# Storing both gates of a token behind its normalised row and fetching them with the gathered row

## The reference

```
x = x + xattn(layernorm(x), ctx, ctx)     # 16 heads of 16, causal without the diagonal
x = x + ffn(layernorm(x))

# ffn: 8 experts, top 2 per token, 512 places per expert
scores = softmax(xt @ wg);  topv, topi = top_k(scores, 2)
topv = topv / sum(topv)                    # the two gates of a token
pos = place of (choice, token) in its expert's queue; valid = pos < 512
disp[topi, pos] += xt * valid
y = relu(disp @ w1 + b1) @ w2 + b2         # per expert, 256 -> 1024 -> 256
out = sum over the two choices of gate * y[topi, pos]
```

## Time and profile before

| | |
|---|---|
| median of three runs | 444.01 us (443.96 to 444.91) |
| profiled execution | 440.71 us |
| its span, first to last instruction | 438.6 us |
| mean granted clock of PE | 0.944 |
| PE busy | 372.2 us (85%), 3042 instructions |
| DVE busy | 292.2 us (67%), 616 instructions |
| ACT busy | 188.9 us (43%), 257 instructions |
| POOL busy | 221.8 us (51%), 306 instructions |
| DMA | 36199 packets, 49.10 MB |

### The profile page before, as it was taken

How to read it: one execution, slowest core, us unless ns; L and a number is a source line. 1 busy time by engine, 2 the same in 40 slices (tenths; PEclk the granted TensorE clock), 3 DMA queues, 4 the chain that set the end, 5 groups by cost and what they waited for, 6 DMA issues and landing times. The chain is left out here.

```text
span 438.6 us, 8178 instructions
## 1 busy us (share of the span) xinstructions
PE 372.2 (85%) x3042; PEld 317.5 (72%) x3062; DVE 292.2 (67%) x616; ACT 188.9 (43%) x257; POOL 221.8 (51%) x306
## 2 busy tenths in 40 slices
PE   3769898989999998876325899999999999999991
PEld 3647586868676766655213799999999998989891
DVE  6676776767676766526564857786776768677840
ACT  4424555555555553552240625344352626262310
POOL 7669766666657563351528703627180817250532
PEclk9988999999999999998655999999999999999997
DMA  8882725151606092214105403728090918230223
GB/s 222 235 235 73 202 61 159 51 169 41 177 8 189 3 240 64 74 73 157 48 1 174 162 2 107 194 63 239 13 272 16 269 31 244 58 46 12 30 31 35
DMA packets 36199, 49.10 MB, mean 112 GB/s; under 512 B 5022, under 2 KB 32064, under 8 KB 35136
## 3 DMA queue, kind: packets, MB, share of 16 engines
q1 hardware_dynamic: 27520, 34.91, 26.7%
q0 software_dynamic: 6144, 8.30, 10.0%
q10 hardware_dynamic: 2496, 5.38, 3.9%
HBM read 27.57 MB, written 8.39 MB: 82 GB/s over the span
## 5 line engine op out<-in xcount | busy, mean ns | idle before, releaser
L1391 POOL DMA_INDIRECT out_dram<-Y,scatter_idx x32 | 51.4, 1605 | 104.0 <-DVE Y L1541 88.3
L1434 ACT ACTIVATE hr<-ps,b_sb 128x512 f32<-128x512 f32 x64 | 43.4, 687 | 101.6 <-PE ps L1601 66.9
L682 DVE TENSOR_REDUCE nm<-ps 128x2 f32<-128x512 f32 (+1 forms) x96 | 61.5, 682 | 16.0 <-remote 10.5
L1611 PE MATMUL ps<-w_hi,h_hi 128*128 128x256 f32 x224 | 63.9, 285 | 1.2 <-DVE h_lo L1509 1.2
L1611 PE MATMUL ps<-w_lo,h_hi 128*128 128x256 f32 x224 | 63.4, 283 | 0.0
L1611 PE MATMUL ps<-w_hi,h_lo 128*128 128x256 f32 x224 | 63.4, 283 | 0.0
L489 ACT ACTIVATE PT<-ps 128x1536 f32<-128x1536 f32 x32 | 46.5, 1452 | 23.5 <-PE ps L936 22.6
L1507 DVE CAST h_hi<-hr 128x512 fp32r<-128x512 f32 x60 | 29.9, 499 | 38.8 <-ACT hr L1434 38.5
L1601 PE MATMUL ps<-XT_hi,w_hi 128*128 128x512 f32 x128 | 51.4, 402 | 1.5 <-DVE XT_lo L1500 1.5
L1601 PE MATMUL ps<-XT_hi,w_lo 128*128 128x512 f32 x128 | 51.2, 400 | 0.0
L1601 PE MATMUL ps<-XT_lo,w_hi 128*128 128x512 f32 x128 | 50.6, 395 | 0.0
(11 more groups left out here) (206 smaller groups left out, 880.6 us busy)
## 6 DMA issues: line engine op xcount, KB each, us to landing
raw<-in_L_ffn_w_dram SPq DMA_DIRECT2D x12, 1024.0 KB, 8.1
raw<-in_L_ffn_w_dram ACTq DMA_DIRECT2D x4, 1024.0 KB, 5.6
Ks<-k_h SPq DMA_DIRECT2D x24, 128.0 KB, 3.0
Qs<-q_h SPq DMA_DIRECT2D x24, 128.0 KB, 2.7
c_sb<-in_ctx_dram SPq DMA_DIRECT2D x8, 256.0 KB, 3.9
Ks<-k_m SPq DMA_DIRECT2D x16, 128.0 KB, 2.8
Qs<-q_m SPq DMA_DIRECT2D x16, 128.0 KB, 2.5
xn_rows<-x2n SPq DMA_DIRECT2D x8, 256.0 KB, 2.5
```

Source lines behind the costliest of these rows:

```text
L682: dve.tensor_reduce(nm[:, tile, h:h + count], max_bank[u % 2].rearrange("p (h j) -> p h j", h=count), AX_X, ALU.max, negate=True).then_inc ...
L1391: pool.indirect_dma_start(out_rows[:, :], bass.IndirectOffsetOnAxis(ap=scatter_idx[:, ST * e + j:ST * e + j + 1], axis=0), Y[q][:, j, :], ...
L1434: act.activation(hr[c % 2][:, :], h_bank[c % 4], ACT.Relu, bias=b1_sb[q][:, c:c + 1]).then_inc(hr_ready, 1)
L1611: last = pe.matmul(y_bank[j // 2][:, (j % 2) * D:(j % 2 + 1) * D], a[c % 4][:, j * P:(j + 1) * P], w[q][:, c, :], start=(c == 0 and n == 0 ...
```

## The change

The row of a token in `xn_rows` gets two more numbers, its two gates, so a row has 258 numbers and `Xg` too. The gates of the first 14 tiles are made and stored in the last step of the first part: ACT's exponential after the rounding of the last attention tile, DVE's three operations between `add_output` and the second `in_slot` piece, and a store on SP behind the last stores of x2n and of the output. The gates of the last two tiles are made at the head of the second part, with two operations on DVE, one on POOL and a store on SP, and POOL's gathers wait for it. A gathered row brings both gates of its token; a table `choice` (full, empty) says which of them holds for a place, and two small DVE operations per expert pick it (`pick_gates`), after the turned rows of that expert. The three parts, `in_gate`, the 32 products and the reduction of their bank go away.

```diff
@@ attention, SP: the last step and the end of the part
-                    sp.dma_start(xn_tiles[s - 1], x2n[:, :, :]).then_inc(x2n_stored, 16)
+                    sp.dma_start(xn_tiles[s - 1][:, :, 0:D], x2n[:, :, :]).then_inc(x2n_stored, 16)
...
             steps(step)
+            sp.wait_ge(gates_ready, 2)
+            sp.dma_start(gate_tiles[:, 0:EARLY, :], gates[:, 0:EARLY, :]).then_inc(gates_stored, 16)
+            sp.wait_ge(gates_stored, 16)
             sp.wait_ge(x2n_stored, 16 * (B + 1))
@@ attention, ACT (called in step B between round_attention and early_rows)
+            def early_ratio():
+                act.wait_ge(top_used, 3 * (B - 1))
+                act.activation(ratio[:, 0:EARLY], dl_all[:, 0:EARLY], ACT.Exp).then_inc(ratio_ready, 1)
@@ attention, DVE (called in step B between add_output and early_slots(0, 1))
+            def early_gates():
+                dve.wait_ge(ratio_ready, 1)
+                then(dve.tensor_scalar(den[:, 0:EARLY], ratio[:, 0:EARLY], 1.0, None, ALU.add))
+                dve.reciprocal(gates[:, 0:EARLY, 0], den[:, 0:EARLY]).then_inc(gates_ready, 1)
+                dve.wait_ge(gates_ready, 1)
+                dve.tensor_tensor(gates[:, 0:EARLY, 1], gates[:, 0:EARLY, 0], ratio[:, 0:EARLY], ALU.mult).then_inc(gates_ready, 1)
@@ experts, SP: ahead of the weight loads
+            sp.wait_ge(gates_ready, 2)
+            sp.dma_start(xn_rows[:, D:D + TOPK].rearrange("(t p) k -> p t k", p=P)[:, EARLY:, :], gates[:, EARLY:, :]).then_inc(gates_stored, 16)
@@ experts, POOL
                     wait_alone(pool, started, xt_done, e - 1)
+                    wait_alone(pool, started, slot_gate_ready, 2 * (e - 1))
...
+            pool.wait_ge(gates_ready, 1)
+            pool.tensor_tensor(gates[:, EARLY:, 1], gates[:, EARLY:, 0], ratio[:, EARLY:], ALU.mult).then_inc(gates_ready, 1)
             pool.wait_ge(placed_b, 1)
...
             pool.tensor_tensor(in_tile[1][:, :, :, :], eq[:, :, EARLY:, :], tiles, ALU.mult).then_inc(placed_k, 1)
+            pool.wait_ge(gates_stored, 16)
             gather(0, 0)
             gather(1, 1)
-            pool.wait_ge(gate_parts, 5)
-            for n in range(3):
-                pool.tensor_tensor(in_gate[:, :, n, :], eq[...], part[:, n, :]..., ALU.mult).then_inc(in_gate_ready, 1)
@@ experts, ACT
-            act.activation(ratio[:, :], dl_all[:, :], ACT.Exp).then_inc(ratio_ready, 1)
+            act.activation(ratio[:, EARLY:], dl_all[:, EARLY:], ACT.Exp).then_inc(ratio_ready, 1)
@@ experts, DVE: after onehot, before the wait for counted
+            dve.wait_ge(ratio_ready, 1)
+            then(dve.tensor_scalar(den[:, EARLY:], ratio[:, EARLY:], 1.0, None, ALU.add))
+            dve.reciprocal(gates[:, EARLY:, 0], den[:, EARLY:]).then_inc(gates_ready, 1)
@@ experts, DVE: after gather_idx
+            dve.tensor_scalar(full, empty, -1.0, 1.0, ALU.mult, ALU.add).then_inc(choice_ready, 1)
@@ experts, DVE: called after every turn_rows(e, q)
+            def pick_gates(e, q):
+                if e >= 1:
+                    dve.wait_ge(slot_gate_ready, 2 * e)
+                dve.wait_ge(choice_ready, 1)
+                for j in range(ST):
+                    dve.wait_ge(gathered[q][j], 16 * (e // 2 + 1))
+                dve.tensor_tensor(picked[:, :, :], Xg[q][:, :, D:], choice[:, ST * e:ST * e + ST, :], ALU.mult).then_inc(slot_gate_ready, 1)
+                dve.wait_ge(slot_gate_ready, 2 * e + 1)
+                dve.tensor_reduce(slot_gate[:, ST * e:ST * e + ST], picked[:, :, :], AX_X, ALU.add).then_inc(slot_gate_ready, 1)
@@ experts, DVE: step, behind the last chunk of expert 0
-                        dve.wait_ge(gate_table_done, 1)
-                        for k in range(TOPK):
-                            dve.tensor_reduce(gate_sum[:, k, :], h_bank[0][...], AX_X, ALU.add).then_inc(slot_gate_ready, 1)
-                        dve.tensor_tensor(gate_two[:, :], empty[:, :], gate_sum[:, 1, :], ALU.mult)...
-                        dve.tensor_tensor(slot_gate[:, :], gate_two[:, :], gate_sum[:, 0, :], ALU.add)...
@@ experts, DVE: after the first weight split
-            then(dve.tensor_scalar(den[:, :], ratio[:, :], 1.0, None, ALU.add))
-            then(dve.reciprocal(gates[:, 0, :], den[:, :]))
-            then(dve.tensor_tensor(gates[:, 1, :], gates[:, 0, :], ratio[:, :], ALU.mult))
-            for n in range(3):
-                dve.tensor_copy(part[:, n, :], left).then_inc(gate_parts, 1)
-                if n < 2:
-                    dve.tensor_tensor(rest[:, n, :], left, part[:, n, :], ALU.subtract).then_inc(gate_parts, 1)
...
@@ experts, PE: expert 0, after the fifth layer 2
-                        pe.wait_ge(in_gate_ready, 3)
-                        pe.wait_ge(hr_ready, 5)
-                        for n in range(KT):
-                            last = pe.matmul(h_bank[0][...], in_slot[:, k, t, :], in_gate[:, n]..., start=(n == 0), stop=True, skip_group_check=True)
-                        last.then_inc(gate_table_done, 1)
@@ program
-        xn_rows = nc.dram_tensor("xn_rows", [T, D], F32, kind="Internal").ap()
+        xn_rows = nc.dram_tensor("xn_rows", [T, D + TOPK], F32, kind="Internal").ap()
```

More of the change, by code:

```diff
@@ L58, in attention @@
     started = persist["started"]
+    ratio, den, gates = (persist[k] for k in ("ratio", "den", "gates"))
     weights_loaded, biases_loaded = persist["weights_loaded"], persist["biases_loaded"]
@@ L217, in weight @@
         return which[:, n].rearrange("p a b -> p (a b)")
+    ratio_ready, gates_ready, gates_stored = (sem(f"early_{n}") for n in ("ratio_ready", "gates_ready", "gates_stored"))
+    gate_tiles = xn_rows[:, D:D + TOPK].rearrange("(t p) k -> p t k", p=P)
     block = nc.Block()
@@ L573, in step @@
                     if s == B:
+                        early_ratio()
                         early_rows()
@@ L822, in step @@
                     add_output(s)
+                    early_gates()
                     early_slots(0, 1)
@@ L1251, in experts @@
     TILES = T // P
-    KT = TOPK * TILES
     EARLY = TILES - 2
@@ L1270, in experts @@
     in_tile = [sb(f"late_in_tile{n}", [P, TOPK, 2, SLOTS], BF16) for n in range(2)]
-    empty = sb("empty", [P, SLOTS], F32)
+    ratio, den, gates = (persist[k] for k in ("ratio", "den", "gates"))
+    choice = sb("choice", [P, SLOTS, TOPK], F32)
+    picked = sb("picked", [P, ST, TOPK], F32)
     second = sb("second", [P, SLOTS], F32)
@@ L1274, in experts @@
     adj = sb("adj", [P, SLOTS], F32)
[L1275 to L1280, removed]
     slot_gate = sb("slot_gate", [P, SLOTS], F32)
@@ L1290, in experts @@
     w2_lo = [sb(f"w2_lo{q}", [P, C, D], F32R) for q in range(2)]
-    Xg = [sb(f"Xg{q}", [P, ST, D], F32) for q in range(2)]
+    Xg = [sb(f"Xg{q}", [P, ST, D + TOPK], F32) for q in range(2)]
     XT_hi = [sb(f"XT_hi{q}", [P, 2, CAP], F32R) for q in range(2)]
@@ L1301, in experts @@
     placed_k, ratio_ready = sem("placed_k"), sem("ratio_ready")
-    gate_parts, in_gate_ready, gate_table_done, slot_gate_ready = (sem(n) for n in ("gate_parts", "in_gate_ready", "gate_table_done", "slot_gate_ready"))
+    gates_ready, gates_stored, choice_ready, slot_gate_ready = (sem(n) for n in ("gates_ready", "gates_stored", "choice_ready", "slot_gate_ready"))
     biased = sem("biased")
@@ L1477, in _ @@
             dve.wait_ge(table_done, 1)
+            empty, full = choice[:, :, 1], choice[:, :, 0]
             first_table, second_table = ps[:, 1, 0:SLOTS], ps[:, 1, SLOTS:2 * SLOTS]
-            then(dve.tensor_scalar(empty[:, :], first_table, 0.0, None, ALU.is_equal))
-            then(dve.tensor_tensor(second[:, :], empty[:, :], second_table, ALU.mult))
+            then(dve.tensor_scalar(empty, first_table, 0.0, None, ALU.is_equal))
+            then(dve.tensor_tensor(second[:, :], empty, second_table, ALU.mult))
             then(dve.tensor_tensor(row[:, :], second[:, :], first_table, ALU.add))
             dve.tensor_scalar(gather_idx[:, :], row[:, :], -float(P), 0.0, ALU.add, ALU.max).then_inc(gidx_ready, 1)
+            dve.tensor_scalar(full, empty, -1.0, 1.0, ALU.mult, ALU.add).then_inc(choice_ready, 1)
             then(dve.tensor_scalar(adj[:, :], row[:, :], 0.0, 1e6, ALU.is_equal, ALU.mult))
@@ L1511, in step @@
                         weights_part(e + 1, 1 - q, c // 2)
-                    if isinstance(e, int) and e < 1 and c == C - 1:
-                        dve.wait_ge(gate_table_done, 1)
-                        for k in range(TOPK):
[L1516 to L1522, removed]
                 if not static(e, E - 1):
                     turn_rows(e + 1, 1 - q)
+                    pick_gates(e + 1, 1 - q)
                 if not (isinstance(e, int) and e < 2):
                     dve.wait_ge(scattered[q], 16 * ST * it)
+                dve.wait_ge(slot_gate_ready, 2 * (e + 1))
                 if e == E - 1:
@@ L1592, in layer1 @@
                         pe.wait_ge(hr_ready, C * e + c - 3)
```

(13 more changed lines are left out.)

9 lines of the change are left out of this document (1 added, 8 removed).

## The result

The kernel after took **438.3 us** in the median of three runs (437.76 to 438.32) against 444.01: a ratio of 0.986, 95% interval 0.984 to 0.989. That is 5.7 us, where 3.3 were forecast and at most 5.0 (439.0) stood in the range.

What follows compares the result with a forecast made beforehand. It took PE alone to bound the kernel from 246 us on, with small DVE operations and POOL gathers before. Terms -1.38 - 1.44 - 0.8 + 0.1 + 0.2 = -3.3 us off 444.01 gave 440.7; range 439.0 to 443.6.

Steps and rivals of the forecast that it cites:

- differences inside its span: Closing step: all terms are differences within the profiled execution's span, so their sum, -3.3 us, comes off the median 444.01.
- x2n's ends: Limits for the last x2n's shift: +0.7 us if DVE's three operations push everything, -2.0 if POOL met no build.
- 32 products and three POOL products: Expert 0: PE's gate products leave the path, -1.38 us; without POOL's in_gate products the h_hi cast shortens, -1.44.
- clock, 0: PE's clock rise at the experts' start keeps its 4.8 us delay: no change, 2.4 us either way at the outside.
- Early gates at the end of the first part: Three DVE operations ahead of an in_slot build let POOL's first two steps through, so x2n starts earlier: -0.8 us.
- Early gates stored: SP's store before the barrier: 112 pieces per engine at 8 ns, 0.9 us, hidden in 2.7 us to spare: 0.
- A: Rival: the early store ends the first part; 47 ns a piece loses 2.6 us, giving 443.3; chance 0.11.
- B: Rival, same store: each piece costs a read and a write, 94 ns, giving 448.5; slower from 54 ns; chance 0.08.
- Late gates: Head of the second part: two short DVE operations between onehot and base cost +0.1 us (0 to 0.4).
- Gathers and picks: Second part: one more DVE operation and rows of 1032 bytes cost +0.2 us (0 to 0.5); the picks nothing.
- C: Rival: POOL's gathers cost more to issue, 0.65 us more for each of four, giving 443.3; chance 0.05.
- D: Rival: moved-up gathers hold the cast, or PE waits elsewhere, so 1.4 us do not come: 442.1; chance 0.09.

Runs made afterwards that it cites:

- two_products: Kernel before with 2 of the 32 gate products on PE, the other 30 left out: 440.19 us, ratio 0.995.
- pool_first: Kernel before with its three POOL products for in_gate put ahead of the gathers for expert 1: 439.34 us, ratio 0.996.
- store_twice: Kernel after with the early gates stored a second time, into an unread table: 9.08 us from x2n to the second part, against 7.18.
- both32: Kernel after with tiles at the old places, w2 and h both 32 B further: 36 products take 4.27 us.
- powers_free: Kernel after with in_slot builds held behind POOL's four steps, second table product behind the router, early gates stored ahead of the last x2n: 433.32 us, ratio 0.980.
- after_moved: Kernel after with the experts' tiles at the addresses of the kernel before: 439.81 us, ratio 0.993.
- first_layer: Kernel before with only w1 and XT moved to their remainders in the kernel after: 440.54 us in a single run.
- w32: Kernel after with tiles at the old places, w2 32 B further, h as before modulo 128: 36 products take 4.28 us, an expert 23.45.
- h32: Kernel after with tiles at the old places, h 32 B further: 36 products take 4.26 us, an expert 23.31.
- before_w64: Kernel before with only w2 moved, 64 B further: 440.02 us, ratio 0.9955.
- before_w96_h32: Kernel before with w2 96 B and h 32 B further: 439.0 us in a single run.
- w64: Kernel after with tiles at the old places, w2 64 B further: 36 products take 4.10 us in five of seven experts, 4.25 in two.
- before_moved: Kernel before with its tiles at the addresses they have in the kernel after: 438.97 us, ratio 0.991.
- second_layer: Kernel before with only w2 and h moved to their remainders in the kernel after: 436.51 us in a single run.

## Why the prediction was wrong

The terms for the edited lines stand in the main; the sum was short of a term.

*The step that failed* is the one that took all terms to be "differences inside its span", at the listed edits, and so left the products of experts 1 to 7 at their durations of before. Removing tiles moves the others, and at the new places of w2 and h the layer-2 products are faster: 3.07 us from the first 36 products on by the chains, and 4.0 to 4.2 us (interval 2.6 to 5.6) by the medians of the moved kernels. Without it the forecast would have held: at the old places the change gave a ratio of 0.993 (0.990 to 0.997), and 440.7 / 444.01 is 0.9925. No term of the sum stood for work that the diff does not touch. The range does not follow from the ends that it names, either: x2n's ends alone give 439.5 to 442.2, and 2.4 us of clock on top would have reached down to 437.1. A range that wide would have held the result by luck.

*32 products and three POOL products*, -1.38 and -1.44, were right in mechanism, each shown alone by two_products and pool_first, and in size. From the end of the third layer-1 chunk to the first 36 products it takes 17.79 us in the kernel before (244.85 to 262.64) and 14.97 in the kernel after at the same places (246.08 to 261.05): 2.82 us, as forecast. The 18 products ahead of that, in which the clock rises, took from 5.84 us (store_twice) to 7.04 (both32) over the executions in which they run without a gap, so *clock, 0* is right only as a middle.

*Early gates at the end of the first part*, -0.8, was the term that was mis-sized: x2n came 0.28 earlier (3.91 to 3.63). The forecast let POOL's first two steps through before the build; DVE's three operations held the build back by 0.55 us (214.59 to 215.14), not the 0.70 that was counted, and the second step and the build began in the same instant. Where POOL is kept clear of it the four steps take 1.75 us from first start to x2n (217.39 to 219.14), the forecast's -2.0 end.

*Early gates stored*, 0, is wrong in mechanism, though it cost little. The pieces did move at about the forecast's price. The DMA rate from 219.8 to 225.6 us, in 40 slices of 0.145 us:

```profile
GB/s 0 0 0 120 332 332 318 374 325 304 219 212 240 367 353 128 13 13 14 14 14 14 10 0 0 0 0 0 0 0 0 0 0 0 0 0 0 56 0 0
```

Behind the two large stores it stands near 14 for seven slices, to about 223.1 us: 1.0 us, or 9 ns for each of an engine's 112 pieces. But the store landed at 225.04 (220.34 + 4.7), some 1.9 us behind its last piece and 2.5 behind the output's store (219.83 + 2.7). The forecast put only 0.9 us of movement against SP's 2.7 us of room, and that room was itself shorter in the changed kernel (2.3 us in powers_free). The Trainium skill, DMA: Bandwidth & Descriptors, Anatomy of one DMA, says that a semaphore moves only when the target memory has confirmed the last byte, and that HBM is the slowest there; it says this of GpSimd's path, and the landing here, on SP's queue, agrees with it. The forecast's own sign of A came true all the same, SP last at the barrier with a wait for the early store, but at 0.12 us against before in place of 2.6, and by the landing, not by the price of a piece. B did not come: at 54 ns a piece the store would have moved for 6 us.

*Late gates*, +0.1, cost nothing: from the second part's first operation to gather_idx it is 4.56 us (225.49 to 230.05), against 4.60 before (222.46 to 227.06). *Gathers and picks*, +0.2, cost about 0.1: from the end of gather_idx to the first product it is 11.12 us (230.23 to 241.35) against 11.01 before. C did not come, for the least gather still takes 0.942 us; nor did D, for no cast exceeds 0.65.

With these sizes, late gates at 0, the change's own terms come to -2.82 - 0.28 + 0.12 + 0.1 = -2.9, and the runs say 3.1 with an interval from 1.5 to 4.7 (0.7% of 443.15, 0.34 to 1.05).

## What to carry to other kernels

When an edit adds, removes or resizes tiles, ask what else moves in memory, and after it compare the mean of unchanged products in unchanged stretches before crediting the edit. A kernel with the old code at the new addresses separates the two, and it needs no more than a few padding tiles. Weigh a DMA that must land against the time to its landing, not only against the time its bytes take.

## What was not expected of the hardware

Layer-2 products of the same shape, at full granted clock and without waits, run at several paces by the places of h and w2:

| remainder of w2 and h, modulo 1024 B | 36 products, us | us per expert |
|---|---|---|
| 640 and 640 (before; after_moved; first_layer) | 4.30 to 4.32 | 23.33 to 23.41 |
| 672 and 768 (w32); 672 and 800 (both32); 640 and 672 (h32) | 4.26 to 4.28, 4.32 once | 23.30 to 23.49 |
| 704 and 640 (before_w64); 736 and 672 (before_w96_h32) | 4.24 to 4.25 | 23.17 to 23.24 |
| 704 and 768 (w64) | 4.09 to 4.10, in two experts 4.25 | 23.05 to 23.22 |
| 992 and 32 (after; before_moved; second_layer) | 4.10 to 4.12, in one expert at times 4.24 | 22.87 to 23.12 |

All kernels that reach 4.10 have 64 B, modulo 128, between h and w2, and so do two that do not; so that distance is not enough, at least not always. What decides between 4.10 and 4.24, even from expert to expert in one run (4.24 in one expert of the kernel after and of second_layer, in none of before_moved and of store_twice, which lie alike), and by what mechanism the place acts at all, stays open.

The cast of 0.43 us was stretched to 3.2 beside POOL's products and came back to at most 0.65 as soon as they lay elsewhere (pool_first); in the other direction, POOL's operations on two columns took up to 1.34 us beside a DVE build and 0.19 to 0.71 clear of it (powers_free).
